# Large attention: values of two key tiles in a row in places; quantised layer: x's scaling on ScalarE

## What is computed

```python
# layer 0, feed-forward: both products take a quantised input
def activation_quant(x):
    scale = 127.0 / jnp.clip(jnp.max(jnp.abs(x), axis=-1, keepdims=True), 1e-05, None)
    return jnp.clip(jnp.round(x * scale), -128, 127) / scale
h = new_gelu(bitlinear(x, w1))        # 256 -> 1024
out = bitlinear(h, w2)                # 1024 -> 256
# layer 1, cross attention: 16 heads, 1601 keys of 64 numbers that all heads share
scores = jnp.einsum('bhsr,bhlr->bhsl', q_r, k_r)
attn = jax.nn.softmax(scores, axis=-1)
ctx_c = jnp.einsum('bhsl,bld->bhsd', attn, kv_r)
...
return ctx @ Wo.T
```

## Time and profile before

| | us |
|---|---|
| median of 3 runs | 2840.44 (2837.37 to 2841.86) |
| the profiled execution | 2837.08, its span 2835.2 |
| PE busy in the span | 2658.0 (94%) |
| DVE, ACT, POOL busy | 1529.4, 1110.6, 1243.3 |
| quantised layer | from about 331 to 465 |
| large attention | from about 466 to 2085 |

### The profile page before, as it was taken

The page is one execution under the profiler, slowest core; times in us unless marked ns, Lnnn a source line. Parts: engine busy times, 40 slices in busy tenths (PEclk is TensorE's granted clock), DMA queues, the critical chain, the costliest instruction groups (busy, mean ns, idle before and its releaser), DMA issues. The chain is left out here.

```text
span 2835.2 us, 46672 instructions
## 1 busy us (share of the span) xinstructions
PE 2658.0 (94%) x16872; PEld 1648.4 (58%) x16872; DVE 1529.4 (54%) x2425; ACT 1110.6 (39%) x2096; POOL 1243.3 (44%) x668
## 2 busy tenths in 40 slices
PE   6989467999999999999999999999979899999999
PEld 4667345656655665666566566656446465656555
DVE  4757585565565556456555655655569633323322
ACT  4635363354445435444543544454435311111110
POOL 1033014577687778668766866776500000000000
PEclk9989698999999999999999999999999899999999
DMA  2000400110111101111110110110030111111111
GB/s 65 1 30 0 153 1 35 50 60 30 47 41 47 41 29 59 38 39 41 47 41 29 59 45 31 41 47 30 18 158 0 32 51 49 56 53 56 52 60 41
DMA packets 44051, 128.00 MB, mean 45 GB/s; under 512 B 6596, under 2 KB 11332, under 8 KB 42312
## 3 DMA queue, kind: packets, MB, share of 16 engines
q1 hardware_dynamic: 43032, 126.53, 13.8%
q10 hardware_dynamic: 944, 0.45, 0.1%
HBM read 85.20 MB, written 2.24 MB: 31 GB/s over the span
## 5 line engine op out<-in xcount | busy, mean ns | idle before, releaser
L716 POOL TENSOR_TENSOR cx_acc<-cx_acc,f_w 128x1024 f32<-128x1024 f32 x310 | 736.4, 2375 | 218.0 <-ACT f_w L1070 205.6
L1070 ACT ACTIVATE f_w<-cx_st 128x512 f32<-128x512 f32 x768 | 438.7, 596 | 447.2 <-PE cx_st L911 392.0
L1174 DVE TENSOR_REDUCE cx_mhalf<-cx_mx 128x1 f32<-128x804 f32 x512 | 480.9, 989 | 171.3 <-PE cx_mx L887 171.2
L922 PE MATMUL cx_av<-f_w,cx_kv 128*64 128x512 f32 x1536 | 412.1, 615 | 0.0
L910 PE MATMUL cx_st<-cx_q,cx_k 128*128 128x512 f32 (+1 forms) x832 | 367.4, 442 | 4.1 <-ACT cx_prob L1070 3.4
L911 PE MATMUL cx_st<-cx_q,cx_k 128*128 128x512 f32 (+1 forms) x832 | 328.9, 395 | 0.0
L887 PE MATMUL cx_mx<-cx_kp,cx_q 128*128 128x402 f32 x1024 | 297.2, 376 | 19.5 <-DVE cx_mhalf L1174 18.3
L887 PEld LDWEIGHTS cx_mx<-cx_kp,cx_q 128*128 128x128 f32 x1024 | 167.6, 189 | 200.2 <-DVE cx_mhalf L1174 183.4
L1996 DVE TENSOR_TENSOR moe_passed<-moe_silu,moe_up 128x512 f32<-128x512 f32 x112 | 76.9, 687 | 382.0 <-issue 356.1
L1917 ACT ACTIVATE moe_silu<-moe_gate 128x512 f32<-128x512 f32 x112 | 66.9, 597 | 490.8 <-PE moe_gate L1841 490.8
L910 PEld LDWEIGHTS cx_st<-cx_q,cx_k 128*128 128x128 f32 (+1 forms) x832 | 154.9, 186 | 170.4 <-ACT f_w L1070 136.4
(11 more groups left out here) (216 smaller groups left out, 3766.3 us busy)
## 6 DMA issues: line engine op xcount, KB each, us to landing
cx_k<-cx_kp SPq DMA_DIRECT2D x32, 804.0 KB, 3.9
moe_share<-moe_coef_kept SPq DMA_DIRECT2D x56, 256.0 KB, 3.0
cx_ctx<-in_cx_ctxN SPq DMA_DIRECT2D x32, 416.0 KB, 3.3
cx_ctxr<-in_cx_ctxrN SPq DMA_DIRECT2D x32, 416.0 KB, 3.9
cx_k<-cx_kp SPq DMA_DIRECT2D x32, 402.0 KB, 5.2
moe_wgu<-in_moe_wgu SPq DMA_DIRECT2D x7, 1024.0 KB, 11.0
moe_wd<-in_moe_wd SPq DMA_DIRECT2D x4, 896.0 KB, 22.3
moe_share<-moe_coef_kept SPq DMA_DIRECT2D x16, 224.0 KB, 2.9
```

The costliest lines, as they stand in the source:

```text
L716: engine.tensor_tensor(acc[rows, :, :], sofar, prob[slot(kt)][rows, :, :], ALU.add).then_inc(s_acc, 1)
L922: last = pe.matmul(av[DCX * p:DCX * p + DCX, :], kv[e][0:nk(kt), kt, :], prob[slot(kt)][0:nk(kt), p, :], start=(kt == 0), stop=(kt == NKT ...
L1070: act.activation(prob[slot(kt)][rows, p, :], st[p][rows, :], ACT.Exp).then_inc(s_exp, 1)
L1174: dve.tensor_reduce(mhalf[:, i // 2, i % 2:i % 2 + 1], mx[i % 2][:, :, 0:KQ], AX.XY, ALU.max)\
```

## The change

In the large attention, PE's `values(n, e, kt)` is issued only for the key tiles in `VALUES_AT[e]`; at such a tile the values of the tile before are issued first, if they were left out. Even batches leave out tiles 2 and 4 (done at 3 and 5), odd ones 5, 7, 9 and 11 (done at 6, 8, 10 and 12). All other orders stay.

In the quantised layer `quantise_x` is cut in three. `find_x_scale` (DVE) normalises, takes the maximum and finds the scale, and stands behind `find_scale`, before `unscale`. `round_x` (ACT, one ACTIVATE with the scale and the rounding constant) replaces DVE's multiply and add, and stands behind the first group of kept weights, before `keep_y2T`. `quantise_x` (DVE) keeps only the last subtraction and clip, and moves to the end of the loop, behind `change_x` and `gather`. At the start both tiles' scales are found first, then both are quantised.

```diff
--- before.py
+++ after.py
@@ -674,6 +674,7 @@
     NEGATE_AT = 9
     ROWS_AT = 11
 
+    VALUES_AT = ((0, 1, 3, 5, 6, 7, 8, 9, 10, 11, 12), (0, 1, 2, 3, 4, 6, 8, 10, 12))
     PIECES_AT = ((0, 0, 1, 3, 3, 5, 4), (0, 0, 0, 0, 0, 3, 3, 3, 3, 4))
 
     def pieces(e, kt, third):
@@ -971,7 +972,10 @@
                         if third == 2:
                             if making and 0 < kt - QUERIES_AT <= CP // 2:
                                 effective(t + 1, 2 * (kt - QUERIES_AT) - 2)
-                            values(n, e, kt)
+                            if kt in VALUES_AT[e]:
+                                if kt - 1 not in VALUES_AT[e] and kt > 0:
+                                    values(n, e, kt - 1)
+                                values(n, e, kt)
                         elif kt + 1 < NKT:
                             scores(n, t, e, kt + 1, third)
                         elif next:
@@ -1418,6 +1422,8 @@
 
     s_var = sem("f0_variance")
     s_rstd = sem("f0_rstd")
+    s_xs = sem("f0_x_scale_found")
+    s_xr = sem("f0_x_rounded")
     s_y1 = sem("f0_y1_quantised")
     s_y1T = sem("f0_y1_turned")
     s_y1Tc = sem("f0_y1T_kept")
@@ -1532,6 +1538,11 @@
                 act.wait_ge(s_y1T, t + 1)
                 act.copy(y1T[t % 2][:, :, :], turned[t % 2][:, 0:DC, :]).then_inc(s_y1Tc, 1)
 
+            def round_x(t):
+                act.wait_ge(s_xs, t + 1)
+                act.activation(xn[t % 2][:, :], xn[t % 2][:, :], ACT.Identity, bias=bias[:, 0:1],
+                               scale=inv[t % 2][:, 0:1]).then_inc(s_xr, 1)
+
             def gelu(t):
                 act.wait_ge(s_hid, t + 1)
                 act.activation(hid[t % 2][:, :], hid[t % 2][:, :], ACT.Gelu_apprx_tanh).then_inc(s_gelu, 1)
@@ -1554,6 +1565,8 @@
                 act.wait_ge(s_made, n + 1)
                 act.copy(kept, made[:, 0:w]).then_inc(s_keep, 1)
 
+            round_x(0)
+            round_x(1)
             keep_y1T(0)
             keep_y1T(1)
             gelu(0)
@@ -1563,6 +1576,8 @@
                     gelu(t + 1)
                 for n in job_range(t, 0):
                     keep(n)
+                if t + 2 < NT:
+                    round_x(t + 2)
                 keep_y2T(t)
                 for n in job_range(t, 1):
                     keep(n)
@@ -1585,18 +1600,23 @@
                 step.done(dve.bn_aggr(mv[t % 2][:, 0:2], stats[t % 2][:, :]))
                 dve.tensor_scalar(mv[t % 2][:, 1:2], mv[t % 2][:, 1:2], EPS, None, ALU.add).then_inc(s_var, 1)
 
-            def quantise_x(t):
+            def find_x_scale(t):
 
                 g = t % 2
                 dve.wait_ge(s_rstd, t + 1)
+                if t >= 2:
+                    dve.wait_ge(s_y1, t - 1)
                 step.done(dve.tensor_scalar(xn[g][:, :], x_all[:, t, :], mv[g][:, 0:1], rstd[g][:, 0:1],
                                             ALU.subtract, ALU.mult))
                 step.done(dve.tensor_reduce(amax[g][:, 0:1], xn[g][:, :], AX.X, ALU.max, apply_absolute_value=True))
-                step.done(scales(t, 0))
-                step.done(dve.tensor_scalar(xn[g][:, :], xn[g][:, :], inv[g][:, 0:1], ROUND, ALU.mult, ALU.add))
+                scales(t, 0).then_inc(s_xs, 1)
+
+            def quantise_x(t):
+                dve.wait_ge(s_xr, t + 1)
                 if t >= 2:
                     dve.wait_ge(s_y1T, t - 1)
-                dve.tensor_scalar(y1[g][:, :], xn[g][:, :], ROUND, 127.0, ALU.subtract, ALU.min).then_inc(s_y1, 1)
+                dve.tensor_scalar(y1[t % 2][:, :], xn[t % 2][:, :], ROUND, 127.0, ALU.subtract, ALU.min)\
+                    .then_inc(s_y1, 1)
 
             def unscale(t):
                 dve.wait_ge(s_up, t + 1)
@@ -1628,21 +1648,25 @@
 
             gather(0)
             gather(1)
+            find_x_scale(0)
+            find_x_scale(1)
             quantise_x(0)
+            quantise_x(1)
             gather(2)
-            quantise_x(1)
             unscale(0)
             for t in range(NT):
                 find_scale(t)
+                if t + 2 < NT:
+                    find_x_scale(t + 2)
                 if t + 1 < NT:
                     unscale(t + 1)
                 quantise_hidden(t)
-                if t + 2 < NT:
-                    quantise_x(t + 2)
                 if t > 0:
                     change_x(t - 1)
                 if t + 3 < NT:
                     gather(t + 3)
+                if t + 2 < NT:
+                    quantise_x(t + 2)
             change_x(NT - 1)
 
 
```

## The result

| | us |
|---|---|
| before, median of 4 runs beside it | 2841.15 (2837.37 to 2843.69) |
| after, median of 4 runs | 2871.23 (2865.66 to 2873.66) |
| ratio after / before | 1.011, 95% interval 1.0093 to 1.0127 |
| the profiled execution of after | 2873.66, its span 2871.9 |

The kernel became slower by 30 us (26 to 36 by the interval), where 31 were forecast. The profiled executions lie 36.7 us apart in span. I cut both spans at the same events: the first instruction of the quantised layer on DVE, the first of the large attention on DVE, and the start of its last output product.

The account below looks back on a forecast made before the run. PE's start-to-start stream was taken to bound the large attention, a chain around three engines the quantised layer. Odd batches 25.2, even 5.0 and last batch 1 gave +31 us, the layer 0: 2840.4 + 31 = 2871, range 2857 to 2883 (0.72).

Parts of the forecast that it names:

- The 0.30 for a merged pair: Attention on PE: two value products in a row save 0.30 us if PE never waits, 28.5 us at most over 95 pairs.
- Tiles 5 and 6, 7 and 8 of odd batches: Odd batches: maximum products wait for DVE's reductions, 6.90 us for 6.63, +0.27 us for each of the two pairs.
- Tiles 9 and 10: Odd batches: about 0.68 us won in tile 9, 0.91 comes back in tile 10, +0.23 us.
- The end of the odd batch: Tiles 11 and 12: PE waits for ACT's exponentials where tile 11's values stood; their deferral costs +0.91 us.
- Rival A: Attention: merges pay, no maximum product waits and tile 11's values' place is free; 28 us less, 2812; chance 0.08.
- B: Attention: only the batch's end hurts, 23 us saved and 14 lost, 2832; chance 0.09.
- C: Attention: only maximum products' waits hurt, tiles 11-12 save 0.30 us; 18 us less than the sum, 2853; chance 0.06.
- Even batches: Attention: tiles 2 and 3 taken as 0, tiles 4 and 5 +0.31 us, 16 times, 5.0 us.
- The last batch: Attention's last batch, without maximum products: ACT's exponentials set the pace, about +0.3 us for each of 3 pairs, 1 us.
- The sign of M's wait: Maximum products' (L887) wait for DVE's reductions in the attention rises from 18 to about 50 us.
- The quantised layer: Steady tiles gain from change_x going first, the start is about 2 us later; sum 0, from -3 to +4 us.
- Rival D: Attention: PE's pause of about 1.3 us per odd batch lowers the clock; 15 falls, 27 us, 2898; chance 0.05.

Follow-up runs that it names:

- odd_end: The kernel before with only tile 11's values held back to tile 12 in odd batches; profiled execution 2856.0 us, attention +13.0 us.
- odd_mid: The kernel before with values of tiles 5, 7 and 9 held back in odd batches only; profiled execution 2853.8 us, attention +10.4 us.
- even_only: The kernel before with values of tiles 2 and 4 held back in even batches only; profiled execution 2845.0 us, attention +2.5 us.
- half_before: The kernel before with each maximum reduction on DVE taken over half of its columns; 2800.57 us in one run.
- attn_only: The kernel before with only the attention's part of the change; 2865.83 us, ratio 1.0095 (1.0072 to 1.0117).
- even_late: The kernel before with values of tiles 7, 9 and 11 held back in even batches only; 2835.48 us, ratio 0.9983 (0.9972 to 0.9995).
- half_after: The kernel before with the change's order of values in both batch kinds and each maximum reduction over half its columns; 2800.34 us in one run.
- ffn_only: The kernel before with only the quantised layer's part of the change; 2839.53 us, ratio 0.9999 (0.9987 to 1.0011).
- change_first: The kernel before with only change_x moved ahead of quantise_x in DVE's order, nothing moved to ACT; 2836.35 us, ratio 0.9982 (0.9967 to 0.9996).

## Why the prediction was right, and where its terms were off

**What bounds the attention.** Right: PE's stream from start to start. `odd_end` and `odd_mid` lengthen the stage by 15 times what they add to an odd batch's distance, to within a us; `even_only` does so only within the 2 us of spread.

**The 0.30 for a merged pair.** Right beside S and M only: 0.24 and 0.25 were measured when nothing waits. The step went wrong as a general price, since it was read from neighbours of one kind. It didn't hurt the sum, as no merge of the change pays in full. Beside the queries' products it is 0.10.

**Tiles 5 and 6, 7 and 8 of odd batches.** Forecast 6.90 for 6.63; measured 6.89. M2 was worked out at 2.17 behind the tile's start and stands at 2.18. The last 0.01 is partly luck: the two V's start at 4.54 for 4.50, and the pair blocks PE for 1.87 (997.87 to 999.74) where I had 0.91 + 1.01 = 1.92. Tiles 7 and 8 +0.27, as forecast. Tiles 9 and 10 +0.16 for +0.23. The part won in tile 9 is right, 0.69 (4.59 before, 3.90 after, from one T to the next) for 0.68. The mis-sized term is the V that comes back in tile 10: 0.84 (2.48 before, 3.32 after, again from T to T) for 0.91.

**The end of the odd batch.** Forecast +0.91, measured +0.83 (6.62 against 5.79 from tile 12's first S to the first S behind the next tile 0), and +0.84 alone in `odd_end`. V11 comes back behind that S, but a pair takes 1.87 there (1019.47 to 1021.34) where V12 alone took 1.01, so it adds 0.86 and not 0.91; I had charged a V of a pair without taking off what the other one saves. Rival A, in which merges pay, is refuted by the sign of the change and by PE's waits. Rivals B and C, which had one of the two causes alone, are refuted: each cause shows by itself.

**Even batches.** Forecast 0 and +0.31: measured 0 (tiles 2 and 3 take 5.95 us in both) and +0.27 (8.75 for 8.48); the whole even batch +0.31.

**The last batch.** Forecast about +0.3 for each pair, measured +0.17. PE's timeline of after, one pair in 4.44 us, where before needed 4.26:

```profile
2080.93 0.50 PE L911 MATMUL cx_st<-cx_q,cx_k 128*128 128x512 f32 x1
...
2082.34 0.50 PE L911 MATMUL cx_st<-cx_q,cx_k 128*128 128x512 f32 x1 [0.22 <-ACT f_w L1074]
...
2083.50 1.94 PE L923 MATMUL cx_av<-f_w,cx_kv 128*64 128x512 f32 x8
2085.37 0.50 PE L911 MATMUL cx_st<-cx_q,cx_k 128*128 128x512 f32 x1
```

The wait is for ACT's exponentials, as said.

**The sum.** 15 x 1.52 = 22.8 for 25.2, 16 x 0.27 = 4.3 for 5.0, the last batch 0.5 for 1: 27.6 for 31; the stage measures 27.1. So the attention was forecast 4 us too high. That the medians lie 30 apart, one from the forecast of 31, is luck for these last us: no term explains why the whole moved by more than the attention did, and the interval of 26 to 36 us holds 27 as well.

**The sign of M's wait.** I said about 50 us and it is 35.0. The direction is right, the size isn't, and the forecast shows no working for it. A step that failed is that it took a wait at the whole delay of M (0.41), while the profile counts as waiting only the part in which PE is idle (0.26 of it before the M at 995.51). Even at 0.41 the 63 new waits would give only 44. The distances, not the sum of waits, are what to price with.

**The quantised layer.** The sum of 0 holds for the whole time (0.9999, within 0.0012). Its terms were worse than that. The steady tile shortened by 0.09 us, not by the 0.2 I had. The mis-sized term is round_x, 0.60 us for the 0.42 I took. ACT's timeline of after, one tile, and the down product on PE that waits for its end:

```profile
371.10 0.46 ACT L1566 COPY cx_wbig<-cx_made 128x384 f32<-128x384 f32 x1
371.46 0.60 ACT L1543 ACTIVATE f_xn<-f_xn,f_round,f_inv 128x256 f32<-128x256 f32 x1
371.96 1.00 ACT L1561 COPY f_y2T<-f_turned 128x1024 bf16<-128x1024 bf16 x1
...
373.02 1.05 PE L1510 MATMUL f_down<-f_w2T,f_y2T 128*128 128x256 bf16 x8 [0.42 <-ACT f_y2T L1561]
```

The releaser of the down product is now ACT, no longer DVE's change_x, as said (the earlier trace rows has DVE). I had chosen by size, near the bf16 copy of 0.37, and should have gone by the operation: its row of 1.24 on 1024 columns has a fixed part that doesn't shrink with the width. The estimate of 0.51 from the Trainium skill (ScalarE: Activation LUTs, Rules for kernel authors) was nearer than mine, and still low; the row it comes from budgets for a bias from a tile, and round_x takes its scale from a tile as well. The advice there, that a multiply or an add belongs on VectorE, agrees with the runs as far as they go: one step of the order alone gives tiles of 6.4 us, and the whole order with the operation on ScalarE 6.90. At the layer's start the loss was 1.7 us, about the 2 forecast.

In the profiled executions, though, the layer took 6.1 us more, beyond my upper bound of 4. The excess lies where the clock was low: from 414 to 450 us it was granted 0.51 on the mean, most of the stretch at 1.2 GHz in place of 2.4, against 0.81 before. Two tiles there took 9.9 and 10.4 us in place of 7.0 and 7.2, and the same two took 9.8 and 9.7 in `half_before`, whose layer is that of before. That isn't a cost of the change that can be read from one pair of profiles. Eight profiled executions hold the layer in the code of before: in four the stretch has 0.81 and the layer takes 133.7 to 134.0 us (before, `attn_only`, `even_late`, `half_after`), in four it has 0.55 or 0.56 and the layer takes 137.9 to 141.4 (`even_only`, `odd_mid`, `odd_end`, `half_before`). The two with the new layer had 0.50 and 0.51, with 139.8 and 143.7. The four low ones were taken together, on one chip, so what that chip did then is as good a cause as chance. Whether the new order makes the low clock likelier stays open with two executions; what it could cost is bounded by `ffn_only`'s interval, 3 us up and 4 down. So the last 9.6 us of the 36.7 between the two profiled spans are this and small differences elsewhere, and the medians, 30 apart, are what the forecast of 31 is to be held against.

**Rival D, the clock in the attention.** Refuted: 15 pauses of 1.23 us, with the granted clock at 1.00 over the stage. The Trainium skill (TensorE: Matmul & The Clock Gate, HAM oscillation) warns of gaps that return in each iteration; the gaps of its own case are longer, and here one of 1.23 us once in 100 us has no such effect.

## What to carry to other kernels

Before an instruction of the bounding engine is put off, ask what ran under it: here most of the V's put off were the time in which VectorE caught up with its reductions, or ScalarE with the exponentials. A merge that saves 0.3 us an instance then costs up to 0.8. Work out two tiles by hand from start-to-start distances, each wait by the end of what it needs; that gave 6.90 where 6.89 was measured. And take a merge's price from the very neighbours that it will have: 0.25 beside one kind was 0.10 beside another.

## What the runs showed of the hardware

- Shortening the reductions from 0.99 to 0.58 us took 41 us off the attention, where PE's waits for them summed to only 18.3. The waits that the profile names were less than half of what their cause cost. Both kernels issue the same 9265 products in this stage in the same order, so their start-to-start distances can be set side by side: 28.7 of the 41 us lie in front of products with a named wait (the profile counts only the idle part of it), 10.3 in front of other M's, and 2 elsewhere. A slower M without a wait looks like this: 0.44 us from the M at 1017.99 in before to its S, 0.36 from the one at 1068.61 in `half_before`.
- The same quantised layer was granted 0.82 of the clock or 0.71 to 0.78, in different kernels that had not touched it, and took 134 or 138 to 141 us. A gain of a few us in such a stage needs many runs: `change_first`'s tile was 8% shorter, and the layer 0.3 us.
- An ACTIVATE with scale and bias from tiles took 0.60 us on 128x256 and 1.24 on 128x1024: a fixed part of some 0.39 us and 0.83 ns a column.
